# Second self attention: the scores are copied out of PSUM by ScalarE before VectorE works on them

## What is computed

```python
qkv = (x @ w_qkv).reshape(B, L, 3, H, D).transpose(2, 0, 3, 1, 4)
q, k, v = (qkv[0], qkv[1], qkv[2])
q = _apply_rope(q, cos, sin)
k = _apply_rope(k, cos, sin)
attn = jnp.einsum('bhqd,bhkd->bhqk', q, k) * scale
attn = jax.nn.softmax(attn, axis=-1)
out = jnp.einsum('bhqk,bhkd->bhqd', attn, v)
out = out.transpose(0, 2, 1, 3).reshape(B, L, C)
return out @ w_proj + b_proj
```

## Time and profile before

| | |
|---|---|
| runs (median, lowest to highest) | 1365.54 us, 1364.18 to 1366.38 |
| the profiled execution | 1366.63 us |
| its span, first to last instruction | 1364.8 us |
| mean granted TensorE clock | 0.937 |
| PE matmul busy | 1233.1 us, 90% |
| DVE busy | 971.8 us, 71% |
| ACT busy | 785.4 us, 58% |
| POOL busy | 636.9 us, 47% |
| second self attention (`self_block`) | about 1217.5 to 1266.0 us |

### The profile page before, as it was taken

How to read it: one execution, slowest core, us unless ns; L and a number is a source line. 1 busy time by engine, 2 the same in 40 slices (tenths; PEclk the granted TensorE clock), 3 DMA queues, 4 the chain that set the end, 5 groups by cost and what they waited for, 6 DMA issues and landing times. The chain is left out here.

```text
span 1364.8 us, 34994 instructions
## 1 busy us (share of the span) xinstructions
PE 1233.1 (90%) x12294; PEld 1037.9 (76%) x12294; DVE 971.8 (71%) x1996; ACT 785.4 (58%) x1435; POOL 636.9 (47%) x581
## 2 busy tenths in 40 slices
PE   5999999999999689639998999999999999777778
PEld 4788888888888549439995788888888888546455
DVE  5767777777777665556626877777777777678896
ACT  3667777777776311115444677777777777224121
POOL 3656656666664305132332666566656654325000
PEclk9999999999999895559999999999999999887899
DMA  7786777777676140534537787776776765100000
GB/s 219 199 207 177 190 197 187 179 194 192 175 177 149 43 62 3 168 116 153 189 140 224 199 203 178 192 193 176 181 206 176 189 169 136 37 0 3 1 8 24
DMA packets 106741, 198.33 MB, mean 145 GB/s; under 512 B 43677, under 2 KB 63806, under 8 KB 106656
## 3 DMA queue, kind: packets, MB, share of 16 engines
q1 hardware_dynamic: 105120, 193.32, 53.9%
q0 software_dynamic: 1536, 3.88, 0.8%
HBM read 88.26 MB, written 10.62 MB: 72 GB/s over the span
## 5 line engine op out<-in xcount | busy, mean ns | idle before, releaser
L900 POOL TENSOR_SCALAR cross_prob<-cross_prob,cross_inverse 128x1024 f32<-128x1024 f32 x256 | 288.7, 1128 | 326.4 <-DVE cross_inverse L634 326.4
L831 ACT ACTIVATE cross_prob<-cross_negated,cross_negmax 128x1024 f32<-128x1024 f32 x256 | 294.9, 1152 | 137.3 <-DVE cross_negmax L626 137.1
L626 DVE CUSTOM_DVE_ANT_0 cross_negated<-cross_scores,cross_bias 128x1024 f32<-128x1024 f32 x256 | 313.6, 1225 | 27.1 <-PE cross_scores L500 8.5
L513 PE MATMUL cross_turn<-ident,cross_prob 128*128 128x128 f32 x2048 | 267.8, 273 | 7.4 <-POOL cross_prob L900 4.4
L513 PEld LDWEIGHTS cross_turn<-ident,cross_prob 128*128 128x128 f32 x2048 | 238.2, 140 | 47.5 <-POOL cross_prob L900 8.7
L840 ACT COPY cross_probT<-cross_turn 128x512 f32<-128x512 f32 x256 | 149.6, 584 | 63.4 <-PE cross_turn L513 62.4
L642 DVE COPY cross_probT<-cross_turn 128x512 f32<-128x512 f32 x256 | 175.5, 686 | 0.0
L500 PE MATMUL cross_scores<-cross_keys,cross_qbd 96*128 96x512 f32 x512 | 170.3, 414 | 3.1 <-POOL cross_qbd L892 3.1
L880 POOL TENSOR_TENSOR cross_ctx_lo<-cross_raw,cross_ctx_hi 128x512 fp32r<-128x512 f32 x120 | 154.8, 1292 | 15.9 <-DVE cross_probT L702 8.3
L443 PE MATMUL cross_out<-cross_wv_hi,cross_ctx_lo 128*128 128x256 f32 x488 | 147.4, 302 | 0.0
L445 PE MATMUL cross_out<-cross_wv_hi,cross_ctx_hi 128*128 128x256 f32 x488 | 137.4, 281 | 0.0
(11 more groups left out here) (283 smaller groups left out, 2126.6 us busy)
## 6 DMA issues: line engine op xcount, KB each, us to landing
cross_keys<-cross_key_hi SPq DMA_DIRECT2D x512, 128.0 KB, 2.4
cross_raw<-in_ctxT SPq DMA_DIRECT2D x32, 1024.0 KB, 5.6
cross_keys<-cross_key_lo SPq DMA_DIRECT2D x256, 128.0 KB, 2.4
cross_bias<-bias_rows SPq DMA_DIRECT2D x32, 512.0 KB, 3.7
up_sb<-in_moe_w SPq DMA_DIRECT2D x8, 1024.0 KB, 9.2
down_sb<-in_moe_w SPq DMA_DIRECT2D x8, 1024.0 KB, 5.8
cross_stacked_q<-q_rows SPq DMA_DIRECT2D x90, 64.0 KB, 2.0
q_rows<-cross_negated SPq DMA_DIRECT2D x8, 256.0 KB, 2.6
```

The costliest lines, as they stand in the source:

```text
L513: last = pe.transpose(ps_t[part][:, k * P:(k + 1) * P], prob[n % 2][:, kt * P:(kt + 1) * P], ident)
L626: dve.tensor_tensor_reduce(negated[n % 2], ps_s[n % 2][:, :], bias_sb[par][:, :], -1.0, 3.0e38, ALU.add, ALU.min, negmax[:, n % 2:n % 2 + ...
L831: act.activation(prob[n % 2][:, :], negated[n % 2], ACT.Exp, bias=negmax[:, n % 2:n % 2 + 1], scale=-1.0, accum_out=total[:, n % 2:n % 2 + ...
L900: pool.tensor_scalar(prob[n % 2][:, :], prob[n % 2][:, :], inverse[:, n % 2:n % 2 + 1], 1.0, ALU.mult, ALU.mult).then_inc(prob_ready, 1)
```

## The change

For layer 1 ACT copies the scores of a step from PSUM to `looked` as soon as PE has written them, and DVE takes the maxima from `looked` and subtracts them there in place. PE's next scores wait for that copy (`seen_copied`) in place of the subtraction. ACT makes the copy for step i+1 ahead of the exponential of step i. Layer 0 runs as it did.

```diff
+        seen_copied = sem("seen_copied") if not by_position else None
...
             def scores(i):
                 a = i % 2
                 pe.wait_ge(qbd_ready, G * (i + 1))
-                if i >= len(score_banks):
-                    pe.wait_ge(shifted, i + 1 - len(score_banks))
+                if by_position and i >= 2:
+                    pe.wait_ge(shifted, i - 1)
+                elif not by_position and i:
+                    pe.wait_ge(seen_copied, i)
...
             def shift(i):
 
                 a = i % 2
-                seen = seen_of(a)
-                dve.wait_ge(scores_ready, i + 1)
-                if i >= 2:
-                    dve.wait_ge(exp_done, i - 1)
+                seen = like(looked[a][:, :, :])
+                if by_position:
+                    dve.wait_ge(scores_ready, i + 1)
+                    if i >= 2:
+                        dve.wait_ge(exp_done, i - 1)
+                else:
+                    dve.wait_ge(seen_copied, i + 1)
...
+            def copy_scores(i):
+
+                act.wait_ge(scores_ready, i + 1)
+                if i >= 2:
+                    act.wait_ge(exp_done, i - 1)
+                act.copy(looked[i % 2][:, :, :].rearrange("p (r m) k -> p r m k", r=4), seen_of(i % 2)).then_inc(seen_copied, 1)
+
+            if not by_position:
+                copy_scores(0)
             for i in range(NT + 3):
+                if not by_position and i + 1 < NT:
+                    copy_scores(i + 1)
                 if i < NT:
                     act.wait_ge(shifted, i + 1)
```

## The result

The changed kernel takes 1369.5 us (median of 12 runs, 1366.86 to 1371.96), the kernel before 1364.43 in as many runs (1363.39 to 1368.01). The ratio of the comparison is 1.0028 with a 95% interval of 1.0018 to 1.0038: 3.8 us slower, 2.5 to 5.2; the two medians lie 5.1 us apart, near the upper end of that. I had forecast +0.8 us, 1366.3, and gave "no change within 0.2%" 0.75. The time lies above the forecast's own range, which ended at 1368.3, and inside only the wider one, which went to 1370.0 where the rivals' times begin. None of the rivals came and no term of my sum led there, so that the wide range holds the time is luck. A small loss was there that I had called no change; "slower" had 0.17, of which 0.14 was for rivals B and C.

The account below looks back on a forecast made before the run. Bound: early loop of scores, maxima, subtraction; later DVE itself. About 3 us gained from the wait is given back by six slower subtractions (one 0.9, five 0.63): +0.8 us, 1366.3 at the median, range 1364.5 to 1368.3.

Parts of the forecast that it names:

- the forecast's own range: Whole kernel: 1364.5 to 1368.3 us, with the clock's rise shifting the before by 1 us and the copy's bounds.
- the wider one: Whole kernel: range to the other cases, 1362.9 to 1370.0 us, leaving out B, C and part of A.
- B: Second self attention: PE stays at 1.2 GHz through the block, so the tail is slower; +7, 1373 us; chance 0.08.
- C: POOL's spreading goes ahead of DVE's subtraction, which waits another 1.19 us in four steps; +4.7, 1371 us; chance 0.06.
- The loop with the subtraction: Early steps: PE's scores no longer wait for maxima and subtraction; maxima 1 at 1225.2 against 1225.59; gain about 3 us.
- The copy on ACT: Eight PSUM-to-SBUF copies of 1.01 us, on the path only in the first two steps, hidden later.
- Maxima from SBUF: DVE's maxima read from SBUF: at most 0.02 us a step gained by the profile rows; nothing taken.
- the advice quoted there: Trainium skill, DVE Perf Modes: copy out of PSUM first where many operations follow; read as making DVE quicker.
- The subtraction: With two SBUF inputs it waits for POOL's instruction, then takes 1.08 us; steady step 4.44 in place of 3.81, +0.63.
- A: Second self attention: no contention between DVE's subtraction and POOL; -2.4 to -3.4 us, 1362.6 at the median; chance 0.12.
- The backlog: POOL's bias additions and third spreading, held up by two subtractions, end at 1229.5 against 1228.75; maxima 2 to 3 takes 4.75.
- The tail is the same on both sides: After the last reciprocal: the last division meets POOL's as before and PE follows, so no time is added.

Follow-up runs that it names:

- the kernel before again: The kernel before, nothing edited, timed against itself as its own comparison: ratio 1.0007 (0.9989 to 1.0024).
- both repairs: Changed kernel with DVE's sums moved between maxima and subtraction and POOL's bias additions moved behind divisions of steps 4 to 6: ratio 0.9988, run again 1.0002.
- half of the change: Changed kernel, but PE's next scores wait for the subtraction as before, not for the copy: 1375.33 us in one run.
- the doubled transposes: Changed kernel with PE making the eight transposes of each of steps 3 to 7 twice: ratio 1.0040 (1.0025 to 1.0055).
- the control: Changed kernel with DVE's sums before the subtraction, POOL's bias additions late, and the transposes of steps 4 and 5 made three times: ratio 1.0007 (0.9989 to 1.0025).

## Why the prediction was off, point by point

*The loop with the subtraction.* Right. Maxima 1 came 6.30 us after the first scores began (forecast 1225.2 - 1218.87 = 6.3), and PE's wait for the subtraction was gone.

*The copy on ACT.* Right: 1.01 us in seven of eight, 1.04 in one. It was on the path once more, before maxima 3, for 0.65 us, since scores 3 were late.

*Maxima from SBUF.* Right that the rows counted: 1190 ns in the mean against 1223, so at most 0.03 us, and no faster mode. That a float32 reduce would be quicker by the advice quoted there was my reading of it; it speaks of elementwise operations.

*The subtraction.* The mechanism is right and shown twice, by taking POOL's reading away (1.22) and by moving it (1.52); the late steps are 4.40 to 4.55 us where I had 4.44. The prediction's rivals A and C fall: with C the subtraction would have been 3 us. One row that I leaned on says more than I read from it: the scalar operation of the first self attention, 0.56 us beside POOL and 0.17 without, has one input only. So one input is no safeguard for every operation; what the runs show free of POOL are the reduces.

*The backlog.* Here the sum's first mistake lies, of 0.8 to 0.9 us. I held up POOL's bias additions by the time the subtractions ran late; but the other side of the contention holds POOL up by about 1 us for each subtraction (2.0 for two in the additions, 0.98 in the first division, 0.97 in a pair). The additions took 2.0 us longer and the third spreading ended at 1232.63, 11.9 after the first scores began, where I had 10.6. The division behind it then fell behind too (2.88), and step 3 took 5.11 us in place of 4.44, step 2 4.91 in place of 4.75. Moving the additions away gave 1.05 us back. I had priced the contention for DVE step by step and for POOL only once.

*"The tail is the same on both sides."* This is the step that failed: 1.4 to 1.5 us. The reason that I gave held, the last division met POOL's as before (1.66 us again), but I took PE's part of the tail to run at the same clock, and PE's early release to cost nothing at the end. With it the scores are done early, the last two rounds have only transposes and weighing, and with DVE's longer steps the projection comes 12 us after the last scores in place of 7.8. The clock fell to 1.2 GHz in that stretch in both profiles. Rival B had the clock as its subject but the wrong stretch: the clock did rise in time, at about 1247.8, and fell later. That the fall costs what the tail lost is shown by PE's rows (1.41 and 1.53 us). That it goes with the change is seen in two profiles of two, with none of two before, and the mean granted clock of all runs agrees: 0.9352 in the twelve of the changed kernel, 0.9388 in the twelve of the kernel before again. Longer steps of DVE are not what it takes, as the clock fell in both repairs too, with steps no longer than before. What exactly lets it fall is not shown.

*Behind the block,* 0.3 to 0.4 us that no step of mine had. DVE's fourth join starts 1.37 us after the third where it was 1.02, and these 0.35 us are about all of it:

```profile
1268.89 0.42 DVE L1246 TENSOR_TENSOR x<-x,self_att_s 128x256 f32<-128x256 f32 x1 [1.29 <-PE self_att_s L1131]
...
1270.26 0.42 DVE L1246 TENSOR_TENSOR x<-x,self_att_s 128x256 f32<-128x256 f32 x1 [0.27 <-issue]
```

The 0.27 us named "issue" is at this place in every kernel made from the changed one, also with DVE's order changed and with half of the change, at full clock, so it goes with neither the clock nor the contention. No experiment tried its cause, and it stays open.

Together: 0.8 forecast, 0.9 for the backlog, 1.4 to 1.5 for the clock and 0.3 to 0.4 behind it make the 3.4 to 3.7 of the profiles.

## What to carry to other kernels

Before you move an operand of a VectorE instruction from PSUM to SBUF, count its SBUF inputs: with two, the subtraction here and the GpSimd instructions that read SBUF held each other up, and both sides have to be priced, in every step. If it must be so, put VectorE's reduces beside GpSimd's long one; here that alone gave back 2.6 us of the block. And where PE is let run ahead, look at what is left for it at the end, since the clock may fall there, as it did here in the changed kernel and not in the kernel before.

## What the runs showed of the hardware

- A VectorE subtraction of 128x1024 took 1.22 to 1.23 us with one SBUF input, or with two beside GpSimd writes, and 1.95 with two beside a GpSimd multiplication that had 0.86 us to go; it ended 1.08 to 1.09 after that.
- The other way round, GpSimd's division took 2.88 us for 1.90 with the end of a subtraction at its start, and a spreading pair 2.16 for 1.19.
- Reduces with one SBUF input were not held up: the maxima took 1.16 to 1.22 beside a division. A scalar operation with one was, in the first self attention: 0.56 us for 0.17.
- At 1.2 GHz a set of eight transposes took 1.97 us against 1.09 at 2.4 GHz. The fall came after rows in which PE was busy part of the time only; an idle stretch of 1.92 us in the kernel before and one of 2.07 with half of the change were not followed by a fall, and one of 1.92 with half of the change and one of 1.73 with the doubled transposes were. In the control idle stretches of at most 0.74 us were not followed by a fall.
- Up to the block, the same program varied by 2.5 to 3.1 us between executions, as much as this change is worth.
